# A graph layer on one core: the products with h of each pair of blocks moved to the end of the step before, and the turn of the sums moved behind the products with agg

## The reference

```
h   = maximum(layernorm(x), 0)                       # 6250 x 128
agg = segment_sum(edge_attr, dst, 6250)              # 6250 x 128, 17 edges a node on average
y   = relu(concat([agg, h], 1) @ W1 + b1)            # W1 256 x 512
out = x + (y @ W2 + b2)                              # W2 512 x 128
```

## Time and profile before

| | us |
|---|---|
| median of three runs (201.18 to 201.53) | 201.28 |
| the profiled execution, its own time | 201.16 |
| its span in the trace | 199.3 |
| TensorE matmul busy | 190.6 |
| TensorE weight load busy | 163.2 |
| VectorE busy | 131.8 |
| ScalarE busy | 86.5 |
| GpSimd busy | 43.4 |

### The profile page before, as it was taken

One profiled execution on the slowest core, in us unless ns is written; L12 is line 12 of the kernel. 1 busy time (PEld: TensorE's weight loads), 2 busy tenths in 40 slices (PEclk: granted clock), 3 DMA queues, 4 the chain that ended last, 5 costly groups with the idle time before them and its releaser, 6 DMA issues.

```text
span 199.3 us, 6821 instructions
## 1 busy us (share of the span) xinstructions
PE 190.6 (96%) x2568; PEld 163.2 (82%) x2568; DVE 131.8 (66%) x582; ACT 86.5 (43%) x188; POOL 43.4 (22%) x119
## 2 busy tenths in 40 slices
PE   7897899998999999999999999999999999999994
PEld 5586789776797898898898898898897898898894
DVE  2865775666877677678568669588487388575221
ACT  3454526433624634623714714813813704823440
POOL 6592202202211202210220220221121121220000
PEclk9999999999999999999999999999999999999999
DMA  6999999999999999999999999999999995010011
GB/s 203 382 374 378 362 373 377 375 375 377 376 377 376 375 379 383 383 392 387 381 378 388 377 385 380 376 385 378 341 376 378 311 376 167 4 53 3 0 53 44
DMA packets 44628, 62.47 MB, mean 313 GB/s; under 512 B 1822, under 2 KB 44300, under 8 KB 44594
## 3 DMA queue, kind: packets, MB, share of 16 engines
q1 hardware_dynamic: 44264, 61.66, 87.2%
q10 hardware_dynamic: 330, 0.36, 0.5%
HBM read 58.81 MB, written 3.20 MB: 311 GB/s over the span
## 4 chain that ended last, share of the span: by engine, by line
PE 79%; DMA 15%; SPq 2%; DVE 1%; issue 1%; DVEq 0%
PE bank L867 21%; PE bank L938 20%; PE bank L907 17%; PE bank L917 15%; DMA edges<-in_edge_attr 15%; PE bank L882 3%; PE bank L891 2%; SPq L303 1%; SPq L297 1%; DVE aggT L623 1%; DVE w_lo L642 0%; PE bank L860 0%; SPq L306 0%; PE bank L837 0%; SPq L327 0%
## 5 line engine op out<-in xcount | busy, mean ns | idle before, releaser
L867 PE MATMUL bank<-edges,onehot 128*32 128x128 f32 x1656 | 52.2, 275 | 2.7 <-DMA edges<-in_edge_attr 1.6
L867 PEld LDWEIGHTS bank<-edges,onehot 128*32 128x32 f32 x1656 | 43.1, 110 | 10.2 <-issue 6.2
L623 DVE TENSOR_TENSOR aggT<-bank,aggT 128x32 f32 x277 | 35.7, 190 | 22.2 <-issue 10.2
L458 ACT ACTIVATE hidden<-bank,b_col 128x512 f32<-128x512 f32 (+2 forms) x56 | 34.2, 634 | 35.9 <-PE bank L917 35.8
L938 PE MATMUL bank<-w,hidden 128*128 128x128 f32 (+1 forms) x392 | 47.6, 278 | 0.0
L938 PEld LDWEIGHTS bank<-w,hidden 128*128 128x128 f32 (+1 forms) x392 | 45.1, 191 | 2.2 <-issue 2.0
L426 ACT ACTIVATE xn<-xs,shift,rstd 128x128 f32<-128x128 f32 (+1 forms) x49 | 21.5, 485 | 49.7 <-POOL shift L383 49.6
L375 POOL TENSOR_SCALAR var<-meanvar 128x2 f32<-128x2 f32 (+1 forms) x25 | 7.9, 317 | 127.4 <-DVE meanvar L559 127.4
L539 DVE TENSOR_TENSOR onehot<-relT,iota 128x384 f32<-128x384 f32 x69 | 34.6, 550 | 0.0
L917 PE MATMUL bank<-agg_hi,w_hi 128*128 128x512 f32 (+2 forms) x56 | 21.5, 385 | 1.4 <-DVE agg_lo L583 1.4
L907 PE MATMUL bank<-hT_hi,w_hi 128*128 128x512 f32 (+2 forms) x56 | 22.2, 396 | 0.3 <-DVE hT_lo L576 0.3
(11 more groups left out here) (104 smaller groups left out, 178.6 us busy)
## 6 DMA issues: line engine op xcount, KB each, us to landing
edges<-in_edge_attr SPq DMA_DIRECT2D x69, 768.0 KB, 10.9
xs<-in_x SPq DMA_DIRECT2D x21, 128.0 KB, 9.8
out_rows<-xs SPq DMA_DIRECT2D x10, 256.0 KB
w<-in_L_gnn_W SPq DMA_DIRECT2D x3, 256.0 KB, 10.5
out_rows<-xs SPq DMA_DIRECT2D x4, 128.0 KB
xs<-in_x SPq DMA_DIRECT2D x1, 256.0 KB, 5.8
hidden<-in_dst SPq DMA_DIRECT2D x1, 192.0 KB, 2.8
hidden<-in_dst ACTq DMA_DIRECT2D x1, 192.0 KB, 4.5
```

The lines of the kernel that those rows point to most:

```text
L458: nc.scalar.activation(hidden[:, t, 0:cols], hidden_of(s, t), ACT.Relu, bias=b1_col[:, t:t + 1]).then_inc(hidden_ready, 1)
L623: nc.vector.tensor_tensor(win, turn_ps[:, at:at + W], win, ALU.add).then_inc(agg_added, 1)
L867: ins = nc.tensor.matmul(sums_ps[t * W:(t + 1) * W, cols], onehot[:, hots, e, :], edges[:, slot, e * F:(e + 1) * F], start=(g == 0), stop= ...
```

## The change

Two things move in TensorE's program; no instruction is added or removed, and the programs of the other engines are the same.

```diff
@@ -1013,19 +1013,20 @@
                     turn_sums(k)
                     turn_x(k + 1)
                     layer1_h(ONES, ONES, 2, 4)
+                elif one is not None:
+                    sum_rounds(k)
+                    turn_x(k + 1)
+                    layer1_agg(one, one, blocks_of(one)[-1] + 1)
+                    turn_sums(k)
                 else:
                     sum_rounds(k)
                     if k == FLAG + 1:
                         pe.wait_ge(over_read, 1)
-                    if two is not None:
-                        layer2(two, two)
-                    if one is not None and one != ONES:
-                        layer1_h(one, one)
+                    layer2(two, two)
                     turn_sums(k)
                     if k + 1 < NB:
                         turn_x(k + 1)
-                    if one is not None:
-                        layer1_agg(one, one, blocks_of(one)[-1] + 1)
+                        layer1_h(group1(k + 1), group1(k + 1))
                 if k == FLAG:
                     pe.wait_ge(overrun_ready, 4)
                     pe.wait_ge(out_added, group1(FLAG))
```

## The result

The changed kernel takes 213.27 us in the median of four runs (212.14 to 213.53), the kernel before 201.41 (201.18 to 201.65, four runs): 1.057 times as long, with a 95% interval of 1.052 to 1.061. It is slower, by the forecast mechanism. The profiled execution took 213.53 us, with a span of 211.8.

What follows compares the result with a forecast made beforehand. TensorE was taken to bound the kernel: 1.07 us by the end of step 7 plus eight pairs of 1.21 (9.68) gave 10.75, less at most 0.2 for the relu, on 201.16: 211.9 us, range 210.5 to 213.4.

Steps and rivals of the forecast that it cites:

- What bounds the kernel: TensorE sets the end from 62 us on; every 0.1 us added in its program after that adds to the time.
- The wait as the profile names it: TensorE waits for agg_lo ten times in odd steps, about 1.1 to 1.2 us each, some 11 us in all.
- The chain of 1.40 us: Odd steps, rounds' end to products with agg: ScalarE's copy of sums, agg_hi, then VectorE's agg_lo; 1.40 us.
- The products with agg with the turn of sums behind them: Odd steps: products 3.02 us including the joint to the rounds, then turn of sums 0.33 us.
- A pair of steps: An odd and an even step take 16.04 us in the changed kernel against 14.83 before, 1.21 more.
- Does the chain start on time?: Odd steps: normalised block, adds into aggT and hT_lo ready before the rounds end, smallest margin 1.4 us; turn of x starts at once.
- rival 3: Chain starts late too, from late adds or normalised block; at 0.3 us in each of nine steps, 214.6 us; chance 6%.
- the forecast's signs of being wrong: agg_hi ahead of the copy, odd-step copy much later than rounds' end, edge wait returning, or turn of x waiting for hT_lo.
- The wait of 0.2 us for the relu: TensorE's one wait for ScalarE's relu goes, as the second layer begins later by the 0.33 us turn of sums.
- The edges: Odd steps' ring slots free later, so loads issue later, costed at nothing; the edge wait at 61.57 us goes.
- Rival 4: Granted clock falls to its lower level for a few us behind each 1.2 us gap; time past 225 us; chance 2%.
- Rival 1, joints only: No new wait before odd steps' products with agg, if the rounding doesn't wait for the copy; 199.7 us; chance 2%.

Runs made afterwards that it cites:

- run 6: Changed kernel with ScalarE copying the sums twice in odd steps from 5 on; 218.69 us, 1.084 to 1.097 of the kernel before.
- run 3: Changed kernel with ScalarE rounding agg (agg_hi) ahead of the copy of sums in odd steps from 5 on; 200.43 us, 0.992 to 0.999 of before.
- run 1: Only half the change: products with h early, turn of sums still ahead of turn of x and products with agg; 209.61 us, 1.035 to 1.045 of before.
- run 5: Changed kernel with six of a pair's twelve products with h put back behind the odd step's rounds; 201.88 us, 0.997 to 1.003 of before.
- run 7: Kernel before with ScalarE copying the sums twice in odd steps from 5 on; 201.55 us, 0.998 to 1.003 of before.
- run 2: Only the other half: turn of sums behind the products with agg in odd steps, products with h unmoved; 201.58 us, 0.996 to 1.002 of before.

## Why the prediction was right, and where it was off

- **What bounds the kernel.** Right. TensorE sets the pace from 62 us on, and the waits put into its program came out in the time: 1.2 us a step by the change, 0.5 more by run 6.
- **The wait as the profile names it.** Forecast were 1.1 to 1.2 us in each of ten waits, some 11 us in all. In the nine steps 7 to 23 the matmuls show 1.0 us each, 9.3 in all, and their weight loads 1.3 each, 11.4 in all; the matmuls of step 5 show only 0.2. The 11.1 us of the first row above agree with the forecast by chance, since steps 1 and 3 are in them.
- **The chain of 1.40 us.** Right, in its members and its length. Between the end of the rounds at 97.51 and the first product with agg at 98.85 lie 1.34 us, with the copy 0.02, agg_hi 0.41 and agg_lo 0.86 behind the end of the rounds; forecast were 0.06, 0.45 and 0.92. In the chain the rounds ahead of a turn of x take 2.15 and not 2.10, and that makes up the difference. Run 6 lengthened it and run 3 took it away; both moved the time as the mechanism says.
- **The products with agg with the turn of sums behind them** took 3.02 + 0.33, as forecast; run 1 confirms the 0.33.
- **The products with h** took 2.78 to 2.80 against 2.77.
- **A pair of steps.** 98.85 to 114.89 is 16.04 us, the forecast's number. From step 5 to step 7 the kernel lost 0.75 us, as forecast (1.07 less the 0.33 of the turn of sums); the eight pairs from step 7 to step 23 grew by 1.25 on average and not by 1.21. So the stretch grew by 11.05 where the sum had 10.75.
- **Does the chain start on time?** Yes, in every step from 7 on: hT_lo and the adds were ready, and rival 3 did not occur there. Step 5 of the profiled execution shows it in small, and with it one of the forecast's signs of being wrong. The turn of x waited 1.0 us for hT_lo; ScalarE, busy with the normalised block and hT_hi, began its copy at 50.07, 0.31 us behind the end of the rounds at 49.76, and the products with agg came 1.62 us behind the rounds and not 1.40. The forecast had taken the start of step 5 as 50.38 in both kernels.
- **The wait of 0.2 us for the relu** was forecast to go, as if it stood in the steps that change. It is in step 24 (194.42 before, 206.45 after), where nothing moved, and stayed; it is too small to see in the time.
- **The edges.** No wait for them behind step 5, as forecast; the holes in the DMA share cost nothing.
- **Clock.** Rival 4, a fall behind the new gaps of 1.0 to 1.2 us, did not happen in steps 5 to 23: the granted clock is 9 tenths or more in every slice but the fifth, and the mean clock of run 6's profiled execution is 1.0, with gaps of up to 1.7 us. The fall in step 1 belongs to the gaps that both kernels have.
- **The size.** 211.9 was forecast, 213.27 measured. The profiled execution, 213.53, is 1.6 us above the forecast. 0.3 of this is the sum itself, and the rest lies outside what the change touches: 1.0 ahead of step 5 (with the clock's fall in step 1), with which I had not reckoned since the profiled execution of before had none, and about 0.5 behind the last addition, less 0.1 in which the trace has no instruction. Against the kernel before, the one execution without the clock's fall is 212.14 - 201.41 = 10.7 us longer.
- **The range** held in part by luck. 213.27 is within 210.5 to 213.4 by 0.13 us, less than the four executions differ among themselves, and the range counted only the chain and the joints, not the start and the end of the program, where most of the miss arose. Worked out again, eight pairs of 1.41 with 1.07 at the start are 12.35 us, and the upper end of the range is 213.5.
- **Rival 1, joints only,** was forecast at 199.7. Run 3 made it real: 200.43 in the median, 200.18 to 200.5 in the six executions without the clock's fall. Its condition was named rightly (the rounding must not wait for the copy), its gain a little too high.

## What to carry to other kernels

Before moving an engine's work away from a place, look up which chain on the other engines that work covers there, end to end and in their queue order: what the moved work leaves behind has to be long enough to cover that chain, and half of it can be as good as all (run 5). An operation whose input has long been there is still late if it stands in its engine's queue behind one that waits; here, exchanging two ScalarE instructions turned a loss of 12 us into a gain of 1. When a sum is laid on one profiled execution, look at the clocks and the spread of several executions before giving its range.

## What the runs showed of the hardware that I had not expected

With two idle gaps of about 0.8 and 1.2 us close together in step 1, the granted clock fell to 0.50 for some 3.5 us in the profiled executions of the changed kernel and of run 7, and also fell behind the gaps of step 1 in runs 2 and 5. With gaps of the same kind (1.12 and 0.87 us) it did not fall in that of the kernel before. By the mean clock of all executions of the unfilled kernels, it falls in about four of ten, with the same program. In the odd steps of the changed kernel, gaps of 1.0 us once in 16 us, with dense work between them, never brought it down. With 28 matmuls of some 0.07 us each in the gaps (0.96 us for 14), none of 30 executions shows a fall.
